# A gated cross-attention block on one core: one product for the last value rows, an output bias added on GpSimd, weights loaded by halves, and calls reordered

## What is computed

```python
# x (4, 1024, 256), ctx (4, 154, 256); _layernorm has no weights
def read(query, mem, top_k=32):
    q, k, v = query @ Wq.T + bq, mem @ Wk.T + bk, mem @ Wv.T + bv
    scores = einsum('btd,bsd->bts', q, k) / sqrt(256)
    vals, idx = top_k(scores, 32)                 # the other scores become -inf
    attn = softmax(masked_to(vals, idx))
    return einsum('bts,bsd->btd', attn, v) @ Wo.T + bo

x = x + tanh(g_xattn) * read(layernorm(x), ctx)
x = x + tanh(g_ffn) * (relu(layernorm(x) @ W1 + b1) @ W2 + b2)
```

## Time and profile before

| | us |
|---|---|
| median of 3 runs | 253.85 |
| lowest and highest | 253.76, 253.93 |
| profiled execution, its own time | 253.36 |
| its span in the profile | 251.3 |

### The profile page before, as it was taken

The page is one execution under the profiler, slowest core; times in us unless marked ns, Lnnn a source line. Parts: engine busy times, 40 slices in busy tenths (PEclk is TensorE's granted clock), DMA queues, the critical chain, the costliest instruction groups (busy, mean ns, idle before and its releaser), DMA issues.

```text
span 251.3 us, 4726 instructions
## 1 busy us (share of the span) xinstructions
PE 246.8 (98%) x1470; PEld 216.9 (86%) x1470; DVE 187.0 (74%) x784; ACT 135.9 (54%) x292; POOL 170.4 (68%) x224
## 2 busy tenths in 40 slices
PE   8999999999999999999999999999999999999995
PEld 7867799999999988898889888898889888988884
DVE  3699999998998993689886988977556969332024
ACT  2579486576657476436660485526661485135720
POOL 3377988997977699674579567873869367745640
PEclk9999999999999999999999999999999999999999
DMA  7993011070301000109112400110011000100202
GB/s 206 379 416 148 0 25 27 1 278 17 125 4 42 0 4 0 42 5 323 52 42 86 126 1 3 42 43 3 0 43 42 3 1 4 39 3 0 83 0 83
DMA packets 6872, 17.21 MB, mean 68 GB/s; under 512 B 800, under 2 KB 2368, under 8 KB 6592
## 3 DMA queue, kind: packets, MB, share of 16 engines
q1 hardware_dynamic: 6848, 16.93, 19.1%
HBM read 12.44 MB, written 4.19 MB: 66 GB/s over the span
## 4 chain that ended last, share of the span: by engine, by line
PE 93%; DVE 5%; issue 1%; ACT 0%; DVEq 0%
PE y_ps L495 24%; PE z_ps L481 12%; PE z_ps L480 12%; PE z_ps L482 12%; PE y_ps L502 12%; PE sc_ps L406 6%; PE pt_ps L427 3%; PE att_ps L448 1%; PE att_ps L461 1%; PE att_ps L445 1%; PE att_ps L447 1%; PE att_ps L446 1%; PE y_ps L308 1%; PE pt_ps L461 1%; DVE picked L1234 1%; PE z_ps L315 1%
## 5 line engine op out<-in xcount | busy, mean ns | idle before, releaser
L1621 POOL TENSOR_TENSOR hid_lo<-hid,hid_hi 128x512 fp32r<-128x512 f32 (+1 forms) x80 | 85.3, 1078 | 50.9 <-ACT hid L960 50.5
L495 PE MATMUL y_ps<-w_both,hid_hi 128*128 128x512 f32 x256 | 83.4, 400 | 0.0
L959 ACT ACTIVATE hid_hi<-z_ps,small_in 128x512 fp32r<-128x512 f32 (+1 forms) x80 | 48.2, 603 | 49.0 <-PE z_ps L482 48.3
L480 PE MATMUL z_ps<-x2nt_hi,w_hi 128*128 128x512 f32 (+1 forms) x160 | 56.7, 354 | 0.0
L481 PE MATMUL z_ps<-x2nt_lo,w_hi 128*128 128x512 f32 (+1 forms) x160 | 55.6, 347 | 0.0
L482 PE MATMUL z_ps<-x2nt_hi,w_lo 128*128 128x512 f32 (+1 forms) x160 | 55.4, 346 | 0.0
L502 PEld LDWEIGHTS y_ps<-w_both,hid_lo 128*128 128x128 f32 x248 | 46.6, 188 | 9.2
L502 PE MATMUL y_ps<-w_both,hid_lo 128*128 128x256 f32 x248 | 52.2, 279 | 0.0
L1292 DVE SCALAR_TENSOR_TENSOR x<-y_ps,tanh_g,x 128x256 f32<-128x256 f32 x64 | 26.8, 477 | 33.4 <-PE y_ps L502 32.4
L960 ACT ACTIVATE hid<-z_ps,small_in 128x512 f32<-128x512 f32 (+1 forms) x80 | 47.9, 599 | 0.0
L495 PEld LDWEIGHTS y_ps<-w_both,hid_hi 128*128 128x128 f32 x256 | 42.7, 188 | 4.0 <-DVE x L1292 0.3
(11 more groups left out here) (147 smaller groups left out, 359.1 us busy)
## 6 DMA issues: line engine op xcount, KB each, us to landing
x_ring<-x SPq DMA_DIRECT2D x8, 512.0 KB, 6.0
out<-x SPq DMA_DIRECT2D x15, 256.0 KB, 2.0
xt_in<-x_t SPq DMA_DIRECT2D x7, 512.0 KB, 4.8
w_in<-w SPq DMA_DIRECT2D x2, 1024.0 KB, 10.5
wkq_in<-w_kq SPq DMA_DIRECT2D x1, 514.0 KB, 3.4
wvo_in<-w_vo SPq DMA_DIRECT2D x1, 513.0 KB, 6.6
xt_in<-x_t SPq DMA_DIRECT2D x2, 256.0 KB, 5.7
ctx_in<-ctx_t SPq DMA_DIRECT2D x1, 462.0 KB, 9.6
```

Source lines behind the costliest of these rows:

```text
L480: mm(dst, w1_hi[:, k, cols], hi[:, k, toks], start=k == 0, stop=False)
L495: last = mm(y_ps[t % 3][:], hid_hi[:, q % RING, tile_of_unit(g, j)], w2_both[:, c, :], start=c == 0, stop=c == KF - 1)
L959: func(hid_hi[:, q % RING, cols], z_ps[q % 2][:, cols], ACT.Relu, bias=b1[:, c:c + 1]).then_inc(hid_hi_made, 1)
L1621: nc.gpsimd.tensor_tensor(hid_lo[:, q % RING, cols], hid[:, q % FULL_RING, cols], hid_hi[:, q % RING, cols], ALU.subtract).then_inc(hid_lo ...
```

## The change

Five things change, all else stays.

- **One product for all rests.** `rest_ctx` holds the last rows of all four batches at distances of 32 (`place_first_rest`, one copy, and `place_other_rests`). `values_of(1)` multiplies it once, `values_of(5)` is gone. `copy_values(1)` writes the high part of batch 0's rest twice (32 rows each), and a new VectorE call, `first_rest_to_lo`, its low part. `move_rests` waits for two copied values instead of six.
- **bo on GpSimd.** `add_wo` adds bo to the one row 0 of the weighed output weights; `fold_value_bias` is one product.
- **Halves of the contraction.** `load_kq(k)` loads the half k of the key and query weights with a semaphore of its own; `fold_queries` multiplies both column halves by the first half before it waits for the second. `multiply_biases` waits for both.
- **Order of the loads.** x(0) and x(1) come before the first piece of the context; w1, w2 and the other context before xt(1).
- **Order of the calls** on all five lists, in the first 60 us above all. GpSimd's `prepare` (the memsets) stands behind `add_wo`, ScalarE's `exps(0, 0)` behind `scale_value_bias`, VectorE's `first_stats_x(0)` ahead of `multiply_biases`, `stats_x(1)` ahead of `scale_scores(0, 0)`.

The diff, cut to its core (of the reordered lists the beginning; behind it calls change places by a few positions):

```diff
-        first_rest = sb("first_rest", [P, KD, P])
-        other_rest = sb("other_rest", [P, KD, P])
+        rest_ctx = sb("rest_ctx", [P, KD, P])
...
             def move_rests():
-                sp.wait_ge(vals_copied, B + 2)
+                sp.wait_ge(vals_copied, 2)
...
-            load_kq()
+            load_kq(0)
+            load_kq(1)
+            load_x(0)
+            load_x(1)
             load_ctx(0)
-            load_x(0)
             load_first_xt()
-            load_second_xt()
             load_vo()
             load_small()
+            load_second_xt()
+            load_ctx(1)
+            load_w1()
+            load_w2()
             load_xt(1)
-            load_w1()
-            load_ctx(1)
-            load_x(1)
-            load_w2()
             load_x(2)
...
-            def fold_queries(m):
-
-                if m == 0:
-                    pe.wait_ge(kq_loaded, 16)
+            def fold_queries():
                 for k in range(KD):
-                    last = mm(z_ps[m][:, 0:D + 1], wk[:, k, m * P:(m + 1) * P], wq_in[:, k, :], start=k == 0, stop=k == KD - 1)
-                last.then_inc(mt_ps_made, 1)
+                    pe.wait_ge(kq_loaded[k], 16)
+                    for m in range(KD):
+                        product = mm(z_ps[m][:, 0:D + 1], wk[:, k, m * P:(m + 1) * P], wq_in[:, k, :], start=k == 0, stop=k == KD - 1)
+                        if k == KD - 1:
+                            product.then_inc(mt_ps_made, 1)
...
             def fold_value_bias():
-                pe.wait_ge(wo_bv_added, 1)
+                pe.wait_ge(wo_bv_added, 2)
                 pe.wait_ge(key_bias_made, 1)
-                mm(y_ps[0][:, 0:D], ones[:], wo_bv[:, 1, :], start=True, stop=False)
-                pe.wait_ge(small_loaded, 16)
-                mm(y_ps[0][:, 0:D], ones[0:1, :], bo[0:1, :], start=False, stop=True).then_inc(value_bias_ps_made, 1)
+                mm(y_ps[0][:, 0:D], ones[:], wo_bv[:, 1, :], start=True, stop=True).then_inc(value_bias_ps_made, 1)
...
 # TensorE's list
             attend(0, 0)
+            scores(1, 0)
             bias_scores(1)
-            scores(1, 0)
             values_of(2)
+            scores(1, 1)
+            transpose_x2n(0, 0)
             values_of(3)
             values_of(4)
-            transpose_x2n(0, 0)
-            scores(1, 1)
-            values_of(5)
             layer_one(0, 0, 0)
             layer_one(0, 0, 1)
             transpose_picked(0, 1)
-            scores(2, 0)
+            layer_one(0, 0, 2)
             layer_two(0, 0, 0)
-            layer_one(0, 0, 2)
             layer_one(0, 0, 3)
+            layer_one(0, 0, 4)
             attend(0, 1)
...
 # ScalarE
+                if n == 1:
+                    func(vals_rest[0:32, 0, :], vals_ps[n][0:32, 0:D], ACT.Copy).then_inc(vals_hi_made, 1)
+                    func(vals_rest[32:64, 0, :], vals_ps[n][0:32, 0:D], ACT.Copy).then_inc(first_rest_repeated, 1)
...
             take_tanh()
-            exps(0, 0)
             fold_wvo()
             scale_value_bias()
+            exps(0, 0)
             copy_values(0)
...
             w1_to_hi(0)
-            w2_to_hi(0)
+            w1_to_hi(1)
+            exps(0, 1)
             copy_keys(1, 0)
-            exps(0, 1)
             copy_keys(1, 1)
...
 # VectorE
+            def first_rest_to_lo():
+                dve.wait_ge(vals_hi_made, 2)
+                dve.wait_ge(vals_copied, 2)
+                nc.vector.tensor_tensor(vals_rest[64:96, 0, :], values[0:32, 1, :], vals_rest[0:32, 0, :],
+                                        ALU.subtract).then_inc(first_rest_lo_made, 1)
...
             prepare()
+            first_stats_x(0)
             multiply_biases()
             centre_queries(0)
             centre_queries(1)
-            first_stats_x(0)
+            first_stats_x(1)
             add_ctx(0)
-            first_stats_x(1)
+            stats_x(1)
             scale_scores(0, 0)
             topk_round(0, 0, 0)
...
             pick(0, 0)
-            stats_x(1)
-            add_ctx(1)
-            pt_to_lo(0, 0)
             scale_scores(0, 1)
             topk_round(0, 1, 0)
+            first_rest_to_lo()
+            pt_to_lo(0, 0)
+            add_ctx(1)
             first_residual()
+            scale_scores(1, 0)
             topk_round(0, 1, 1)
-            scale_scores(1, 0)
             normalise_second()
...
             pt_to_lo(0, 1)
-            stats_x(2)
-            residual(0, 1)
             topk_round(1, 0, 2)
             topk_round(1, 0, 3)
+            residual(0, 1)
+            topk_round(1, 1, 0)
             pick(1, 0)
-            topk_round(1, 1, 0)
+            stats_x(2)
             x2nt_to_lo(0, 1)
...
 # GpSimd
+                pool.wait_ge(wo_bv_added, 1)
+                pool.wait_ge(small_loaded, 16)
+                nc.gpsimd.tensor_tensor(wo_bv[0:1, 1, :], wo_bv[0:1, 1, :], bo[0:1, :], ALU.add).then_inc(wo_bv_added, 1)
+                pool.wait_ge(wo_bv_added, 2)
...
-            prepare()
             rstd_x(0, 0)
             add_wo()
-            stack_first_rest()
-            scale_b2()
+            prepare()
+            place_first_rest()
+            place_other_rests()
             value_bias_to_lo()
             rstd_x(0, 1)
-            place_other_rests()
+            rstd_x(1)
             first_values_to_lo()
-            rstd_x(1)
             w1_to_lo(0)
             normalise_x2(0, 0)
             w1_to_lo(1)
             w2_to_lo(0)
             w2_to_lo(1)
             hid_to_lo(0, 0, 0)
+            w2_to_lo(2)
             hid_to_lo(0, 0, 1)
-            w2_to_lo(2)
-            w2_to_lo(3)
             hid_to_lo(0, 0, 2)
```

452 lines of the change are left out of this document (222 added, 230 removed).

## The result

The changed kernel takes 259.73 us (median of six, 258.46 to 260.23) against 253.81 us (253.06 to 254.31): 5.9 us more between the medians. The ratio is 1.0225, 2.25% more, with a 95% interval of 1.0194 to 1.0256. The prediction said 253.65 us, no change as the likeliest, and a range that ended at 255.2.

A forecast was written before the change was run, and what follows sets the result against it. VectorE and what it waits for were taken to set the pace before about 35 us, TensorE alone behind; +0.2 us at 13.8 us, -0.3 by 35 us, +0.1 behind gave -0.2, a median of 253.65 us, range 252.2 to 255.2.

The forecast's parts named there:

- What bounds the kernel: Whole kernel: before about 35 us VectorE and what it waits for set the pace, behind it TensorE alone.
- Products that go, bo on GpSimd: TensorE loses 1.39 and 0.62 us of products, 2.0 together; GpSimd's added instruction takes 0.73 us, hidden by 0.4 us.
- Weights by halves: Folding at 4.18 us: no gain; a loss of 0.2 us if the second half lands after 5.0 us.
- Order of loads: First loads: x(0) lands at 5.5 us, x(1) at 6.8, first ctx piece at 8.1, the other at 13.5.
- VectorE's start: Centring queued behind first_stats_x(0): TensorE loses 0.95 us, of which 0.62 and some 0.1 come back at the bias stage.
- Up to the first attention: From the bias stage to the first attention: released at 20.95 us, where VectorE's instruction at 20.82 us stood before.
- From there to 45 us: First attention to 45 us: transposes start 0.45 us earlier, 0.3 us ahead at attend(0, 1), 0.1 us lost at pick(1, 0).
- second rival: At add_ctx(1): GpSimd wins the exclusion, add_ctx(1) stands for 2.38 us; 255.05 us, chance 0.20.
- forecast's own case: At pick(0, 1): the pick meets both w2_to_lo, two instructions over 1 us; median 253.65 us, chance 0.43.
- first rival: At pick(0, 1): pick's first instruction is issued ahead of w2_to_lo, ending one GpSimd instruction earlier; 252.5 us, chance 0.27.
- Behind 45 us: Calls only change places: gain bounded by 0.2 us, an early call can cost 0 to 0.5 us; taken as 0.
- fourth rival: Behind 45 us: a call placed too early makes the kernel slower; 254.3 us, chance 0.06.

The follow-up runs named there:

- e5: Changed kernel with first context and x(0) loaded ahead of x(1), context first, and first_stats_x(0) behind centre_queries(1) again; 256.32 us, ratio to before 1.0106.
- e6: e5 with the order of the kernel before on all five engines behind a cut at 85 to 95 us; 254.95 us, ratio to before 1.0053.
- e10: Order of the kernel before with merged product and bo on GpSimd, other context loaded earlier, weights in two halves, old folding loop; 254.08 us, ratio 1.0026.
- e9: Kernel before with key and query weights loaded as two halves and fold_queries looping over the contraction outside; 254.01 us, ratio to before 1.0009.
- e12: e6 with fold_queries finishing one output block after the other and add_ctx(0) ahead of first_stats_x(1); 255.10 us, ratio to before 1.0062.
- e1: Changed kernel with VectorE's first_stats_x(0) behind centre_queries(1) again, loads as changed; 257.50 us, ratio to before 1.0141.
- e3: Changed kernel with seven more products of ones in TensorE's two waits of the first 10 us; 257.37 us, ratio to before 1.0158.
- e4: Kernel before with VectorE's first_stats_x(0) moved ahead of multiply_biases, nothing else changed; 256.30 us, ratio to before 1.0116.
- e8: Kernel before up to a cut at 85 to 95 us, the changed kernel's order behind it; 258.13 us, ratio to before 1.0156.
- e15: Kernel before with GpSimd's w2_to_lo(1), (2) and (3) moved behind hid_to_lo(0,0,1), (0,0,3) and (0,0,5); 253.43 us, ratio to before 0.9985.
- e17: Kernel before with GpSimd's one-source scale_b2 moved between w2_to_lo(0) and w2_to_lo(1); 253.16 us, ratio to before 0.9981.
- e13: e5 with three VectorE calls, pt_to_lo(4,0), pt_to_lo(5,0) and output(4,0), moved back in front of what was put ahead of them; 259.89 us, ratio to before 1.0220.
- e14: e5 with pick reading one SBUF tile instead of two from the fifth group on; 255.62 us, ratio to before 1.0063.
- e11: e5 with GpSimd's hid_to_lo reading one tile instead of two; 259.59 us, ratio to before 1.0250.

## Why the prediction was wrong, step by step

By the ratios the 2.25% split so: the start 1.19 (e5), the late order 0.53 (e6), the merged product with bo 0.26 (e10), the halves 0.09 (e9, not clear of zero); 0.18 are left. The 0.6 us that e6 loses at the cut are 0.23 points, so the late order is rather worth 0.76, and nothing is left for the order between 12 and 85 us. Each of these figures is uncertain by 0.1 to 0.6 points. Three steps of the prediction failed: the landing of x(0) and with it the start, the clock, which was no term at all, and the late order, which was put at 0.

*What bounds the kernel.* Right, and not taken seriously enough. The prediction said that VectorE sets the pace before 35 us; e10 shows that this covers the whole of the removed 2.0 us of products: it has them gone and is no faster.

*Products that go, bo on GpSimd.* Sizes right. The addition took 0.63 us (0.73 forecast), and `fold_value_bias` had no wait in the changed kernel, where TensorE came 3 us late. The forecast cover of 0.4 us is not there when TensorE is on time: e10 and e12 wait 0.46 us for the addition, which is the "up to 0.5 us" that the step named. Value of both zero.

*Weights by halves.* "No gain", with a loss only if the second half came late. The step looked at the landing and not at the loop: turning the loops round delays the first finished block. 0.31 us in the trace.

*Order of loads.* Failed. x(0) was put at 5.5 us by counting bytes in a row, and landed at 7.31; x(1) at 8.61 (6.8 forecast), the first context at 9.09 (8.1), the others at 13.84 (13.5). In e1 and e3, with the same loads, x(0) landed at 7.78 and 7.77 us; behind the context instead of ahead of it at 7.28 (e5) and 6.88 (e6). The place on the queue was worth little of what the sum gave it. The halves may have their part in this: behind one whole load of the weights and the context, x(0) landed at 6.78 to 7.21 us in five profiles (before, e4, e8, e15, e17), behind two halves and the context at 6.88 to 8.65 in eleven, 8.0 in the median. No run splits this load with nothing else changed on TensorE, so its price in time is open.

*VectorE's start.* The mechanism was right and the largest term was mis-sized: a loss of 0.95 us forecast, 2.50 measured at `make_keys(0, 0)`. The landing of x(0), 1.8 us later than forecast, covers the 1.55 us between. The wait at `bk_bq` was not in the sum at all; it adds nothing to the start of `make_keys`, which waits for the centring anyway, but it is one of the two waits ahead of the fall of the clock. That the bias stage would give 0.62 and some back was right (`fold_value_bias` took 0.43 us, no wait).

*The clock.* Missing. A wait of TensorE was priced at its length. Here two waits were followed by 5 us at a mean clock of 0.66, and e3 puts that at 1.4 us in the profiled executions and 1.7 us by the ratios.

*Up to the first attention.* 20.95 forecast, 23.86 measured. Of the 2.9 us between, 1.55 are the start and, by e3, about 1.4 the clock. The third copy on ScalarE was left out and `first_rest_to_lo` was taken as hidden; e10 has them on the path, with 0.42 us at most.

*From there to 45 us.* Right to 0.1 us in both halves: 10.12 against 10.05 us to the transposes, and 0.25 us won back over before where 0.3 was forecast. The second rival didn't happen (`add_ctx(1)` took 0.70 us at 23.84). So the forecast's own case, two long pick instructions, came true here. The first rival is real, and a matter of chance: in e5 the pick starts at 28.68 and the `w2_to_lo` at 28.67 us, and its two instructions take 1.45 and 1.38 us; in e13, same calls up to there, both engines start at 28.89 us, the first instruction takes 0.31 us and the second 1.40, and 22.00 us instead of 23.24 pass from `attend(0, 0)` to `layer_one(0, 1, 0)`.

*Behind 45 us.* Failed, and by the prediction's own sign: it was to be wrong "if TensorE stands after 45 us". "TensorE has no hole there that a new order could fill" is true of the gain, not of the loss, and the loss was priced at 0 to 0.5 us and taken as 0, without looking at what VectorE would have ahead of each `pt_to_lo` and each `output`. It measured 2.36 us. The fourth rival was this mechanism, with a chance of 0.06 and a quarter of its size. That the late order costs it is shown (e8, e6, and the waits in every profile). The mechanism has two halves: a pick stretched beside `hid_to_lo`, and a place on VectorE ahead of what TensorE waits for. e14 shows that the stretch reaches TensorE one for one, e13 that a wait goes when the order alone is changed. What remains open is which order would lose nothing: e13's opened a longer wait.

## What to carry to other kernels

Before pricing removed work, ask which engine sets the pace at the place where it stood; here work removed from an engine that waits there was worth nothing, and work added to the ones it waits for made it wait longer. Whatever waits for a transfer at the head of an in-order engine holds up every small instruction behind it, and on TensorE such a wait can cost more than its length, since the clock may fall behind it (0.66 and 0.50 here). Where the busiest engine has no idle time a new order can only lose: check each engine's queue ahead of what the busiest engine awaits, not the busiest engine's share.

## What the runs showed of the hardware

The eight instructions of the folding, the same work in every kernel, took 1.90 to 3.41 us over the twenty profiles, 2.30 in the one of before. One of the long ones, in e12:

```profile
4.19 3.33 PE L317 MATMUL z_ps<-wkq_in 128*128 128x257 f32 x8
```

In the slow ones the first ones start 0.43 us apart and the later ones 0.22 us, a ratio of two, and the place of the change differs from run to run; the granted clock reads 1.00 in the whole stretch, so the table doesn't show it. It comes in kernels with either order (e17, which folds as before, 3.08 us) and so is no effect of the change, but it is up to 1.5 us at the head of the chain, and single profiles of the start must not be compared by absolute times.

A pick (VectorE, two SBUF inputs) that starts in the middle of a two-source GpSimd instruction on 128x256 or 128x512 ends 0.17 or 0.18 us behind it (ten instructions in the kernel before). Beside GpSimd's small two-source instruction on 128x2 it isn't held (0.31 us at 71.36 us in before). Who starts first wins: a GpSimd start 0.01 us earlier held the pick for 1.45 us (e5), with both starts at 28.89 us the pick took 0.31 us (e13). These are two single events. One-source GpSimd instructions let the pick through mostly (sixteen of twenty in e11 at 0.31 to 0.33 us, the longest 0.757). The other way round, a small one-source GpSimd instruction was held beside a VectorE instruction with two SBUF inputs.
